# A graph layer's message stage: two tiles of three added on VectorE instead of one of two

## The chip, the cores and the metric

The kernel runs on one core of a Trainium2 chip. The metric is the device time of one execution in microseconds (us), as a median over runs. The engines that matter here are TensorE (PE in the profile; PEld is its weight load), VectorE (DVE), ScalarE (ACT), GpSimd (POOL) and SyncE (SP), which issues transfers.

## The reference

Four blocks follow each other: a relational graph layer pair, a mixture-of-experts block, four graph layers with batch normalization, and a quantized feed-forward block. The change touches the third block alone, of which each layer is

```python
e = edge_attr @ We + be                      # 5000 edges x 512
m = relu(x[src] + e)                         # gather of rows of x, one for each edge
agg = segment_sum(m, dst, num_segments=x.shape[0])
h = ((1.0 + eps) * x + agg) @ W1 + b1
... batch norm, relu, @ W2, relu
```

It runs over 10,000 nodes, 512 features, 5,000 edges, and four layers.

## The kernel before

Each of the four layers is three phases with barriers of all engines between them: `message_phase` (the edges: `m`, and its sums over edges of equal target), `hidden_phase` and `output_phase`. The layers are built as a first one, an inner one that a loop runs twice, and a final one. Edges are sorted by target and cut into `ET` = 40 tiles of 128.

In `message_phase`, for tile t:

- GpSimd gathers 128 rows of the table into `x[t % 8]` (L1820). It waits until tile t-8 has been summed.
- TensorE makes the edge terms in a PSUM bank `X[t % 4]`: a product of 5 rows, `kept_edge_terms` by `kept_attr_terms` (L1904). For a tile that is `summed`, it adds the gathered rows by a second product with the identity matrix (L1912). In the profile that product has two records for each tile.
- For a tile that is not `summed`, VectorE adds bank and gathered rows into an SBUF buffer `z` (`add`, L1849).
- ScalarE takes relu, rounded for TensorE, into `mh` (`high`, L1878). VectorE makes the remainder `ml` (`low`, L1854).
- TensorE multiplies both with a selection matrix into `B` (`sums`, L1920 and L1921), ScalarE copies to `res` (L1883), and SyncE stores `res` and its first and last row (L1804, L1805).

The first layer (`normal`) sums all tiles on TensorE. In the later three, even tiles are `summed`. Every engine works through its own list in program order, which `static_pipeline` writes: at turn t TensorE issues `attr(t)`, then `sums(t - 2)`; VectorE `add(t)`, then `low(t - 1)`; ScalarE `high(t)`, then `result(t - 2)`. TensorE's `sums(t)` waits for `ml` of tile t. After tile 20 ScalarE and after tile 24 VectorE also split the next weights (L717, L721).

`output_phase` of one layer loads the selection matrices and edge terms of the next one ahead, into space that its own big tile has freed. `TERMS_AT`, from `MESSAGE_ROWS`, says from which group of rows on that space is free.

Of the kernel before, what the change touches and what calls it, by code (L numbers as in the profile page):

```python
# [10 lines left out]
P = 128  # L11
N, D, E = 10000, 512, 5000
# [1708 lines left out]
    return v.rearrange(f"one {names} -> (one {names.split()[0]}) {' '.join(names.split()[1:])}")  # L1721


MESSAGE_ROWS = 10
TERMS_AT = (EP + MESSAGE_ROWS * D) - N


# [17 lines left out]
def message_phase(core, ed, table, layer, weight, ident, half, normal, kept, ahead):  # L1745
# [6 lines left out]
    W, R, XR = 4, 8, 4  # L1752
    CHUNK = 5
    HEAD = XR * P
    SPLIT_AT = ET // 2
    summed = lambda t: normal or t % 2 == 0
    of_pe = lambda t: sum(summed(k) for k in range(t + 1))
    of_dve = lambda t: max(0, t + 1) - of_pe(t)
    names = ("w whi wlo terms more sel0 sel1 sel2 sel3 sel4 sel5 sel6 sel7 E X z mh ml B res zero H hres done st0 st1 st2 st3 "
             "bn aggr var rstd nb nx xin swg0 swg1 swg2 swg3 swg4 swg5 swg6 swg7")  # L1760
    with core.phase("message", names) as (s, sbuf, psum):
# [2 lines left out]
        select, edge_terms, attr_terms = kept  # L1764
        sbuf("select", [P, ET, P], F32R)
        x = [sbuf(f"x{q}", [P, D]) for q in range(R)]
        z = [sbuf(f"z{q}", [P, D]) for q in range(2)]
        sbuf("edge_terms", [TERMS, EP], F32R), sbuf("attr_terms", [TERMS, D], F32R)
        borders = sbuf("borders", [EDGE_ROWS, D])
        mh = [sbuf(f"mh{q}", [P, D], F32R) for q in range(W)]  # L1770
# [5 lines left out]
        X = [psum(f"X{q}", [P, D]) for q in range(XR)]  # L1776
        B = [psum(f"B{q}", [P, D]) for q in range(2)]
        H = psum("H", [ET, D])
        ga, st = [s[f"swg{q}"] for q in range(R)], [s[f"st{q}"] for q in range(W)]
        sum_of = lambda t: X[t % XR] if summed(t) else z[t // 2 % 2]  # L1780

        def wait_sum(eng, t):

# [884 lines left out]
def second_gnn(core, cst, ed, a, g, skip, rows_out, stats, rowst):  # L2668
# [3 lines left out]
    with nc.sbuf_tensor("kept_below", [P, 3 * KC, D], F32), nc.sbuf_tensor("kept_select", [P, ET, P], F32R) as select, \  # L2672
            nc.sbuf_tensor("kept_between", [P, MESSAGE_ROWS, D], F32), nc.sbuf_tensor("kept_edge_terms", [TERMS, EP], F32R) as edge_terms, \
            nc.sbuf_tensor("kept_attr_terms", [TERMS, D], F32R) as attr_terms:
        kept = select, edge_terms, attr_terms

    def one_layer(layer, first, final):
        table = skip if first else g
        name = "first" if first else "final" if final else "inner"

        def weight(name):
            return a[name][bass.ds(layer, 1)].rearrange("one (c p) n -> (one p) c n", p=P)

        with nc.sbuf_tensor(f"layer_hi_{name}", [P, KC, D], F32R) as hi, nc.sbuf_tensor(f"layer_lo_{name}", [P, KC, D], F32R) as lo, \
                nc.sbuf_tensor(f"layer_raw_{name}", [P, KC, D], F32) as raw:
            message_phase(core, ed, table, layer, (raw, weight("L1_gnn_W1"), hi, lo), cst.ident, cst.half, first, kept, not first)
            with nc.sbuf_tensor(f"hT_{name}", [P, KC, N], F32) as hT:
                hidden_phase(core, cst, ed, table, a["L1_gnn_eps"], a["L1_gnn_b1"], (raw, weight("L1_gnn_W2"), hi, lo), layer, hT, stats, first)
                affine = a["L1_gnn_gamma"], a["L1_gnn_beta"], a["L1_gnn_b2"]
                if final:  # L2690
                    last_output_phase(core, cst, rows_out, skip, *affine, (raw, hi, lo), layer, hT, stats, rowst)
                else:
                    output_phase(core, cst, ed, g, *affine, (raw, hi, lo), layer, hT, stats, kept)
# [65 lines left out]
```

## Time and profile before

| what | value |
|---|---|
| median of three runs | 4840.01 us (4828.76 to 4846.31) |
| the profiled execution's own time | 4834.37 us |
| its span | 4832.6 us |
| mean granted TensorE clock | 0.897 |
| busy share of PE, DVE, ACT, POOL | 87%, 60%, 43%, 25% |

The three message stages of later layers lie at about 2824 to 2911, 3433 to 3512 and 4030 to 4112 us of the span. A row of a timeline gives start, duration, engine, line, tile names, and in brackets the idle time before it and what ended it. A row of windows gives the busy time of each engine in that stretch, then the granted clock, then the busy share of the transfer engines. A granted clock of 1.00 is 2.4 GHz, and 0.50 is 1.2 GHz, the only two levels seen; a value between them is a mean.

### The profile page before, as it was taken

To read this page: it belongs to the slowest core of one execution; us is meant where nothing else is said; L and a number is where in the kernel's file an instruction comes from. 1 tells how busy PE (TensorE), PEld (TensorE's weight loads), DVE (VectorE), ACT (ScalarE), POOL (GpSimd) and SP (SyncE) were. 2 spreads that over 40 slices of the span, in tenths; PEclk is the share of its full clock that TensorE was granted. 3 is DMA by queue.
4 is the path that set the end of the run, shared out by engine and by line. 5 is a ranking of instruction groups with operands and counts; after the bars stand their busy time and mean duration, and the time that the engine had idled before them with its cause. 6 is when DMAs were issued, how large, how long until landed. Compare 5 with 4: busy or idle time off the path is not lost. (4 is left out here: it accounts for less than half of the span.)

```text
span 4832.6 us, 65959 instructions
## 1 busy us (share of the span) xinstructions
PE 4200.5 (87%) x22921; PEld 3391.4 (70%) x22921; DVE 2883.9 (60%) x6014; ACT 2057.0 (43%) x3499; POOL 1206.0 (25%) x1230
## 2 busy tenths in 40 slices
PE   7868979899898954868899998999889998899967
PEld 4437867778786843653898847988589884898844
DVE  5547743377586766755785444544445444456888
ACT  1212212222233622426556753357533575334556
POOL 2431112211242002875441033300333003330010
PEclk9989989999998966877899989999999998999965
DMA  9982248622598933986442364423655236544677
GB/s 344 399 281 98 74 147 267 223 91 75 200 407 327 346 123 85 175 150 207 150 156 87 117 199 161 163 88 110 212 167 161 85 114 206 168 158 131 186 192 214
DMA packets 454538, 875.49 MB, mean 181 GB/s; under 512 B 69409, under 2 KB 109969, under 8 KB 453486
## 3 DMA queue, kind: packets, MB, share of 16 engines
q1 hardware_dynamic: 305049, 528.82, 32.0%
q0 software_dynamic: 77312, 227.96, 16.7%
q10 hardware_dynamic: 71912, 115.30, 7.1%
q8 instruction: 152, 2.49, 0.2%
q14 instruction: 113, 0.92, 0.1%
HBM read 567.94 MB, written 302.99 MB: 180 GB/s over the span
## 5 line engine op out<-in xcount | busy, mean ns | idle before, releaser
L1974 POOL DMA_INDIRECT hidden_agg<-edge_sums,edge_where x316 | 355.1, 1124 | 702.7 <-DVE layer_raw_inner L2060 288.1
L731 PE MATMUL hidden_O<-hidden_xh,layer_hi_inner 128*128 128x256 f32 (+1 forms) x1280 | 367.9, 287 | 0.0
L733 PE MATMUL hidden_O<-hidden_xl,layer_hi_inner 128*128 128x256 f32 (+1 forms) x1280 | 361.8, 283 | 0.0
L732 PE MATMUL hidden_O<-hidden_xh,layer_lo_inner 128*128 128x256 f32 (+1 forms) x1280 | 361.2, 282 | 0.0
L1820 POOL DMA_INDIRECT message_x<-g,edge_partner x120 | 116.6, 972 | 777.4 <-POOLq L147 461.8
L731 PE MATMUL output_O<-layer_hi_inner,output_hh 128*128 128x512 f32 (+1 forms) x632 | 251.7, 398 | 18.4 <-DVE output_hl L2154 18.4
L2017 ACT ACTIVATE hT_inner<-hidden_O,hidden_b 128x256 f32<-128x256 f32 (+1 forms) x320 | 123.9, 470 | 332.4 <-PE hidden_O L733 332.4
L731 PE MATMUL root_O<-root_hi,root_xh 128*128 128x512 f32 (+1 forms) x632 | 255.8, 405 | 0.0
L731 PE MATMUL relation_B<-relation_weights,relation_pth 128*128 128x512 f32 x640 | 253.7, 396 | 0.0
L732 PE MATMUL relation_B<-relation_weights,relation_ptl 128*128 128x512 f32 x640 | 253.5, 396 | 0.0
L733 PE MATMUL relation_B<-relation_weights,relation_pth 128*128 128x512 f32 x640 | 253.3, 396 | 0.0
L732 PE MATMUL output_O<-layer_hi_inner,output_hl 128*128 128x512 f32 (+1 forms) x632 | 251.3, 398 | 0.0
L733 PE MATMUL output_O<-layer_lo_inner,output_hh 128*128 128x512 f32 (+1 forms) x632 | 251.1, 397 | 0.0
L733 PE MATMUL root_O<-root_lo,root_xh 128*128 128x512 f32 (+1 forms) x632 | 249.0, 394 | 0.0
L732 PE MATMUL root_O<-root_hi,root_xl 128*128 128x512 f32 (+1 forms) x632 | 248.2, 393 | 0.0
L2163 DVE TENSOR_TENSOR layer_raw_inner<-output_O,output_b2t 128x1024 f32<-128x1024 f32 x80 | 96.9, 1211 | 249.9 <-PE output_O L733 249.9
L732 PEld LDWEIGHTS hidden_O<-hidden_xh,layer_lo_inner 128*128 128x128 f32 x1280 | 243.8, 190 | 0.0
L731 PEld LDWEIGHTS hidden_O<-hidden_xh,layer_hi_inner 128*128 128x128 f32 x1280 | 243.5, 190 | 0.2 <-DVE hidden_xl L1104 0.2
L733 PEld LDWEIGHTS hidden_O<-hidden_xl,layer_hi_inner 128*128 128x128 f32 x1280 | 243.5, 190 | 0.0
L1098 ACT ACTIVATE root_xh<-root_T 128x1024 fp32r<-128x1024 f32 x80 | 80.5, 1007 | 348.3 <-PE root_T L987 348.3
L1009 POOL DMA_INDIRECT root_agg<-edge_sums,edge_where x158 | 152.0, 962 | 285.9 <-DVE root_y L1061 173.7
L2072 DVE BATCH_NORM_STATS2 h_stats<-hT_inner 128x6 f32<-128x512 f32 (+2 forms) x168 | 97.6, 644 | 168.4 <-ACT hT_inner L2017 168.4
(464 smaller groups left out, 12723.3 us busy)
## 6 DMA issues: line engine op xcount, KB each, us to landing
edge_sums<-message_res SPq DMA_DIRECT2D x160, 256.0 KB
layer_raw_inner<-g SPq DMA_DIRECT2D x78, 512.0 KB, 3.9
g<-layer_raw_inner SPq DMA_DIRECT2D x78, 512.0 KB
room<-in_L_gnn_basis SPq DMA_DIRECT2D x30, 1280.0 KB, 14.7
order_basis<-in_L_gnn_basis SPq DMA_DIRECT2D x18, 1280.0 KB, 14.2
edge_sums<-relation_res SPq DMA_DIRECT2D x80, 256.0 KB
order_x<-in_x SPq DMA_DIRECT2D x39, 512.0 KB
normed<-order_y ACTq DMA_DIRECT2D x39, 512.0 KB
```

Source lines behind the costliest of these rows:

```text
L731: eng.matmul(out, a_hi, b_hi, start=start, stop=False)
L732: eng.matmul(out, a_lo, b_hi, start=False, stop=False)
L733: return eng.matmul(out, a_hi, b_lo, start=False, stop=stop)
L1009: eng.indirect_dma_start(agg[q][0:n, t, :], None, ed.sums[0], bass.IndirectOffsetOnAxis(ap=ed.where[0][0:n, j:j + 1], axis=0)).then_inc(ga ...
L1098: eng.activation(xh[q][:, :, 0:w], T[q][:, :, 0:w], ACT.Copy).then_inc(s["hi"], 1)
L1820: eng.indirect_dma_start(x[t % R][:, :], None, table, bass.IndirectOffsetOnAxis(ap=ed.partner[1][:, t:t + 1], axis=0)).then_inc(ga[t % R], 16)
L1974: eng.indirect_dma_start(agg[j % R][0:n, :], None, ed.sums[1], bass.IndirectOffsetOnAxis(ap=ed.where[1][0:n, c:c + 1], axis=0)).then_inc(g ...
L2017: m = eng.activation(hT[:, o, at(g)], O[g % 2][:, o, 0:width_of(last(g))], ACT.Identity, bias=b1t[:, o:o + 1])
L2072: eng.bn_stats(stats[:, o, g // 2 + last(g), :], hT[:, o, (g if g in alone else g - 1) * GROUP:at(g).stop]).then_inc(s["bn"], 1)
L2163: eng.tensor_tensor(part(y[q], last), part(O[q], last), b2t[0:n, :].unsqueeze(1).to_broadcast([n, k, D]), ALU.add).then_inc(s["add"], 1)
```

## The change

Of the tiles of later layers only every third is `summed` on TensorE. VectorE adds two of three: 26 tiles instead of 20 in each of the three stages, and TensorE makes 14 identity products instead of 20. A third buffer `z` is added, with its ring counted by the number of adds, and `MESSAGE_ROWS` grows by the one row of space that it takes.

```diff
-MESSAGE_ROWS = 10
+MESSAGE_ROWS = 11
 TERMS_AT = (EP + MESSAGE_ROWS * D) - N
...
-    summed = lambda t: normal or t % 2 == 0
+    summed = lambda t: normal or t % 3 == 0
     of_pe = lambda t: sum(summed(k) for k in range(t + 1))
     of_dve = lambda t: max(0, t + 1) - of_pe(t)
...
-        z = [sbuf(f"z{q}", [P, D]) for q in range(2)]
+        z = [sbuf(f"z{q}", [P, D]) for q in range(3)]
...
-        sum_of = lambda t: X[t % XR] if summed(t) else z[t // 2 % 2]
+        sum_of = lambda t: X[t % XR] if summed(t) else z[(of_dve(t) - 1) % 3]
```

TensorE in the inner layer's message stage before, from `attr(12)` on; the digit behind a name is its buffer, so `X0` is the bank of tiles 12 and 16, and `B0` takes even tiles.

```order
L1904 MATMUL message13_X0<-kept_attr_terms,kept_edge_terms 128x512
L1912 MATMUL message13_X0<-message13_x4,cst_ident 128x512
L1920 MATMUL message13_B0<-message13_mh2,kept_select 128x512
L1921 MATMUL message13_B0<-message13_ml2,kept_select 128x512
L1904 MATMUL message13_X1<-kept_attr_terms,kept_edge_terms 128x512
L1920 MATMUL message13_B1<-message13_mh3,kept_select 128x512
L1921 MATMUL message13_B1<-message13_ml3,kept_select 128x512
L1904 MATMUL message13_X2<-kept_attr_terms,kept_edge_terms 128x512
L1912 MATMUL message13_X2<-message13_x6,cst_ident 128x512
L1920 MATMUL message13_B0<-message13_mh0,kept_select 128x512
```

The same place in the changed kernel:

```order
L1904 MATMUL message13_X0<-kept_attr_terms,kept_edge_terms 128x512
L1912 MATMUL message13_X0<-message13_x4,cst_ident 128x512
L1920 MATMUL message13_B0<-message13_mh2,kept_select 128x512
L1921 MATMUL message13_B0<-message13_ml2,kept_select 128x512
L1904 MATMUL message13_X1<-kept_attr_terms,kept_edge_terms 128x512
L1920 MATMUL message13_B1<-message13_mh3,kept_select 128x512
L1921 MATMUL message13_B1<-message13_ml3,kept_select 128x512
L1904 MATMUL message13_X2<-kept_attr_terms,kept_edge_terms 128x512
L1920 MATMUL message13_B0<-message13_mh0,kept_select 128x512
L1921 MATMUL message13_B0<-message13_ml0,kept_select 128x512
L1904 MATMUL message13_X3<-kept_attr_terms,kept_edge_terms 128x512
L1912 MATMUL message13_X3<-message13_x7,cst_ident 128x512
```

The identity product of tile 14 is gone, and `B0<-mh0`, the sums of the `summed` tile 12, now stand right behind `attr(14)`.

VectorE at the same place before, from the add of tile 13 on (`z0` is tile 13, `ml0` tile 12):

```order
L1849 TENSOR_TENSOR message13_z0<-message13_X1,message13_x5 128x512
L1854 SCALAR_TENSOR_TENSOR message13_ml0<-message13_X0,message13_mh0 128x512
L1854 SCALAR_TENSOR_TENSOR message13_ml1<-message13_z0,message13_mh1 128x512
L1849 TENSOR_TENSOR message13_z1<-message13_X3,message13_x7 128x512
L1854 SCALAR_TENSOR_TENSOR message13_ml2<-message13_X2,message13_mh2 128x512
```

And in the changed kernel, from the add of tile 13 on (`z2` is tile 13, `z0` tile 14):

```order
L1849 TENSOR_TENSOR message13_z2<-message13_X1,message13_x5 128x512
L1854 SCALAR_TENSOR_TENSOR message13_ml0<-message13_X0,message13_mh0 128x512
L1849 TENSOR_TENSOR message13_z0<-message13_X2,message13_x6 128x512
L1854 SCALAR_TENSOR_TENSOR message13_ml1<-message13_z2,message13_mh1 128x512
L1854 SCALAR_TENSOR_TENSOR message13_ml2<-message13_z0,message13_mh2 128x512
```

In both the `low` of the `summed` tile 12 stands behind the add of tile 13. An add of tile 14 is new behind it.

## Rows read from the trace of the kernel before

**Rows 1.** The page: span, and granted clock in 40 slices.

```profile
span 4832.6 us, 65959 instructions
...
PEclk9989989999998966877899989999999998999965
```

**Rows 2.** Windows: the three message stages, from first identity product to last sums.

```profile
2831.00:2910.00 79.00, 76.42 (x159) 32.16 (x159) 41.70 (x61) 46.15 (x80) 33.89 (x36) 0.77 0.77 248
3442.00:3510.00 68.00, 65.12 (x157) 27.75 (x155) 41.55 (x61) 45.13 (x79) 31.93 (x33) 0.91 0.84 280
4035.00:4111.00 76.00, 71.71 (x158) 30.44 (x158) 41.79 (x61) 44.92 (x80) 35.44 (x37) 0.82 0.81 263
```

**Rows 3.** Timeline of PE, two tiles at a granted clock of 1.00.

```profile
3499.31 0.49 PE L1904 MATMUL message_X<-kept_attr_terms,kept_edge_terms 5*128 5x512 f32 x1
...
3500.29 0.79 PE L1920 MATMUL message_B<-message_mh,kept_select 128*128 128x512 f32 x1
...
3501.25 0.50 PE L1904 MATMUL message_X<-kept_attr_terms,kept_edge_terms 5*128 5x512 f32 x1
3501.68 0.50 PE L1920 MATMUL message_B<-message_mh,kept_select 128*128 128x512 f32 x1
...
3502.34 0.49 PE L1904 MATMUL message_X<-kept_attr_terms,kept_edge_terms 5*128 5x512 f32 x1
```

**Rows 4.** Timeline of PE, two tiles at a granted clock of 0.50.

```profile
2842.27 0.79 PE L1904 MATMUL message_X<-kept_attr_terms,kept_edge_terms 5*128 5x512 f32 x1
2842.99 0.80 PE L1920 MATMUL message_B<-message_mh,kept_select 128*128 128x512 f32 x1
...
2844.14 0.79 PE L1904 MATMUL message_X<-kept_attr_terms,kept_edge_terms 5*128 5x512 f32 x1
2844.87 2.08 PE L1912 MATMUL message_X<-message_x,cst_ident 128*128 128x512 f32 x2
...
2847.73 0.79 PE L1904 MATMUL message_X<-kept_attr_terms,kept_edge_terms 5*128 5x512 f32 x1
```

**Rows 5.** Timeline of PE, end of the final layer's stage, after `attr(39)`.

```profile
4108.21 0.49 PE L1904 MATMUL message_X<-kept_attr_terms,kept_edge_terms 5*128 5x512 f32 x1
4108.63 0.50 PE L1920 MATMUL message_B<-message_mh,kept_select 128*128 128x512 f32 x1
...
4110.14 0.50 PE L1920 MATMUL message_B<-message_mh,kept_select 128*128 128x512 f32 x1 [0.77 <-DVE message_ml L1854]
```

**Rows 6.** Timeline of DVE, at the places of rows 5.

```profile
4108.80 0.69 DVE L1849 TENSOR_TENSOR message_z<-message_X,message_x 128x512 f32<-128x512 f32 x1 [1.07 <-PE message_X L1904]
4109.40 0.68 DVE L1854 SCALAR_TENSOR_TENSOR message_ml<-message_X,message_mh 128x512 fp32r<-128x512 f32 x1
```

**Rows 7.** Timeline of DVE, at the places of rows 4.

```profile
2843.16 0.69 DVE L1849 TENSOR_TENSOR message_z<-message_X,message_x 128x512 f32<-128x512 f32 x1 [3.36 <-PE message_X L1904]
2843.76 0.68 DVE L1854 SCALAR_TENSOR_TENSOR message_ml<-message_X,message_mh 128x512 fp32r<-128x512 f32 x1
```

**Rows 8.** Windows: a stretch at either level, inside the first stage of rows 2.

```profile
2832.00:2853.00 21.00, 21.00 (x32) 8.36 (x30) 7.97 (x12) 8.72 (x15) 10.09 (x12) 0.50 0.76 220
2861.00:2872.00 11.00, 10.57 (x30) 4.67 (x29) 7.05 (x11) 7.68 (x15) 6.74 (x8) 1.00 0.97 339
```

**Rows 9.** Timeline of PE, where the granted clock falls in the first stage.

```profile
2878.99 0.50 PE L1920 MATMUL message_B<-message_mh,kept_select 128*128 128x512 f32 x1 [0.43 <-DVE message_ml L1854]
...
2882.98 0.51 PE L1920 MATMUL message_B<-message_mh,kept_select 128*128 128x512 f32 x1 [0.89 <-DVE message_ml L1854]
...
2884.07 1.76 PE L1912 MATMUL message_X<-message_x,cst_ident 128*128 128x512 f32 x2
```

**Rows 10.** Windows: after that fall, and the end of the final layer's stage.

```profile
2885.00:2897.00 12.00, 12.00 (x19) 4.93 (x18) 3.96 (x6) 4.84 (x9) 3.78 (x4) 0.50 0.75 220
...
4104.00:4112.00 8.00, 5.74 (x16) 2.41 (x15) 4.06 (x6) 5.67 (x11) 0.00 (x0) 1.00 0.45 173
```

**Rows 11.** Windows: the first layer's message stage, all tiles summed on PE.

```profile
2191.00:2239.00 48.00, 48.00 (x66) 18.95 (x66) 23.81 (x71) 25.17 (x40) 23.94 (x31) 0.50 0.53 183
2239.00:2291.00 52.00, 51.51 (x134) 22.87 (x133) 41.24 (x120) 46.42 (x79) 31.54 (x42) 1.00 0.72 235
```

**Rows 12.** Timeline of SP's queue, end of an output phase.

```profile
3394.84 0.29 SPq L1738 DMA_DIRECT2D kept_attr_terms<-edge_attr_rows  x1
3399.78 30.05 SPq L2114 DMA_DIRECT2D g<-layer_raw_inner  x7
```

## The prediction

> **What bounds the stage now.** I read the page first, then windows over the three stages that the change touches, then the timelines of TensorE and VectorE inside them. The page gives a span of 4832.6 us and a granted clock that changes from slice to slice [rows 1]. The three message stages of later layers last 79, 68 and 76 us, 223 us in all, 4.6% of the span, so nothing else is at stake [rows 2]. In them TensorE is busy nearly throughout (76.4 of 79 us in the first), VectorE a little over half. TensorE sets the pace: two tiles take 3.03 us at a granted clock of 1.00 (from `attr` at 3499.31 to that at 3502.34) and 5.46 us at 0.50 (2842.27 to 2847.73) [rows 3, 4]. The stages differ in length only by their mean clocks of 0.77, 0.91 and 0.82. Time at 0.50 is twice the missing share: 79 x 2 x 0.23 = 36 us, 12 and 27, together 76 us, or 76 / 2.73 = 28 of 120 tiles. The other 92 at 1.515 us need 139 us. 223 - 76 - 139 leaves 8 us of waits.
>
> **What is removed.** Six identity products in each stage, 18 in all. At 1.00 a tile with one takes 1.94 us (3499.31 to 3501.25) and one without 1.09 (to 3502.34) [rows 3]; at 0.50 it is 3.59 (2844.14 to 2847.73) and 1.87 us (2842.27 to 2844.14) [rows 4]. So a product is worth 0.85 us at the upper level and 1.72 at the lower, and TensorE's own work for three tiles falls from 4.55 to 4.12 us, or from 8.19 to 7.33.
>
> **What is added: a wait at the upper level.** Eighteen adds on VectorE cost 0.69 us each, and VectorE has room. The place decides. `low` of a `summed` tile stands behind the add of the tile after it, which waits for that tile's `attr` product. TensorE's sums of the `summed` tile wait for this `low`. Before, an identity product stood between and hid the detour. Now only `attr` does: from `attr(13)` to `sums(12)` there are one tile without identity (1.09 us) and one `attr` (3501.25 to 3501.68, 0.43), 1.52 us. The trace of before has this pattern once in each stage, at its end, where no identity product follows `attr(39)`. There the add starts 0.59 us after `attr` (4108.21, 4108.80), `low` 0.60 later, it lasts 0.68, and TensorE goes on at 4110.14 [rows 5, 6]: 1.93 us from `attr` to the sums. 1.93 - 1.52 = 0.41 us of waiting in each three tiles, so they take 4.12 + 0.41 = 4.53 us. Before it was 4.55. **At the upper level the gain is nil** (0.02 us for three tiles, under 1 us over all).
>
> At the lower level the add starts 0.89 us after `attr` (2842.27, 2843.16) and `low` 0.60 later [rows 4, 7]; with 0.68 and 0.06 us that is 2.23 us, and TensorE has 1.87 + 0.72 = 2.59 us of its own work in between. No wait: three tiles take 7.33 instead of 8.19 us, a gain of 0.29 us a tile.
>
> The second add and the two `low` behind it end before TensorE needs them, since the next identity product lies ahead. ScalarE's work per tile is unchanged (45 us of 68 busy [rows 2]). Gathers are released by the add or the sum eight tiles earlier, in the same order as before.
>
> Transfers would stop a gain at the upper level even without the wait. Their busy share is 0.97 at 1.00 and 0.76 at 0.50 [rows 8]; at the lower level a tile in 2.44 instead of 2.73 us makes it 0.85, so there is room there.
>
> **The moved loads.** `TERMS_AT` moves the ten loads of the next stage two groups later. Before, seven stores follow the last load, over 30 us (3394.84, 3399.78 to 3429.8) [rows 12]; five will, over some 20 us. They stay hidden behind TensorE's work; uncovered, the delay could cost at most two groups, some 10 us, in three places.
>
> **The clock.** With the clock as before, the sum is 28 x 0.29 = 8 us gained. But the change alters what the clock answers to. In the first stage the clock is 1.00 until TensorE waits 0.43 us and then 0.89 us for `ml`, four microseconds apart; in the next identity product it is 0.50 (the record stretches to 1.76 us), and then it stays there for over 12 us, although TensorE shows no idle time at all [rows 9, 10]. After the change a wait of 0.41 us comes back every 4.53 us through the whole upper level, and the identity product, the longest stretch of unbroken streaming, comes once in 4.53 us instead of once in 3.03. At the lower level it comes once in 7.33 instead of 5.46 us. So I expect it to fall more readily and rise more reluctantly. How reluctant a rise can be shows the first layer: 48 us at 0.50 with TensorE busy without a gap [rows 11].
>
> I put H for the tiles at the lower level. The three stages take 8 + 120 x 1.51 + H x (2.44 - 1.51) us = 189 + 0.93 H. H = 28, as before, gives 215 us, a change of -8. H = 120, never up, gives 301, +78. H = 0 gives -34. Even is H = 37. The rows do not fix H: the fall of rows 9 followed a wait twice as long as the new one, but one such wait and not one every 4.5 us; rises came within 12 us in the second stage (all that it spent at 0.50), after over 21 in the first and after 48 in the first layer [rows 2, 8, 11]. I choose the middle between as before and never up, H = 74: 258 us, +35 us. The profiled execution took 4834.4 us, so 4869 us. Its time lies 6 us under the median shown, inside the runs' spread of 18 us.
>
> The Trainium skill ("TensorE: Matmul & The Clock Gate", section "HAM oscillation") lets the clock fall where matmuls wait long for a transfer and holds it up otherwise; by that rule waits of 0.41 us would cost nothing, and the time would be that of the rival below with the clock as before. The trace disagrees in part: two short waits sufficed. A neighbouring section ("A second HAM failure mode: psum-queue depth-cycling") has short frequent idles between groups of matmuls making it swing, which is my forecast.
>
> **The rivals.**
> - **The clock keeps its pattern.** H stays near 28: -8 us, 4826; with H of 20 to 50, -15 to +13. For it: in the last 8 us of the final stage TensorE is busy for 5.74 us only, with a wait of 0.77 us, and the clock stays 1.00 [rows 10]. Against it: the stretch is short and ends the stage.
> - **The wait does not come, and the clock holds**, the case on the other side. If `low` of the `summed` tile reached TensorE in time, three tiles would take 4.12 us at the upper level, 0.14 us a tile less: 92 x 0.14 = 13 us, with the 8 us of the lower level 21, so 4813 us. It decides if the detour through `attr(13)` is under 1.52 us. Rows 5 and 6 give 1.93, and transfers at 0.97 stand against it too.
> - **The clock never rises.** H = 120, +78 us, 4912. For it: the first layer's 48 us. Against it: all three stages of before rose, with mean clocks of 0.77 and more [rows 2].
>
> **How the numbers follow.** A measurement of this kernel tells about 0.5% from no change, 24 us around 4840. Chances: clock lower for more tiles, H from 50 to 110 (+13 to +68), 0.56; clock as before 0.32; no wait 0.08; never up 0.04. Slower by over 0.5% means over 4864, H above 69: about seven tenths of the first case and all of the last, 0.43. Faster needs under 4816: most of the no-wait case, 0.07. The rest, 0.50, is within 0.5%. The range goes from the clock kept (4826) to H = 110 (4902). The likeliest case alone spans 4847 to 4902.
>
> **What the profile after would show.** At 1.00, TensorE's sums behind the `attr` of a tile t with t mod 3 = 2 wait 0.4 us for L1854, and three tiles take 4.5 us. At 0.50 they take 7.3 us without a wait. The identity product has 82 calls (164 records) in place of 100, VectorE 78 adds in place of 60. The three stages have mean clocks of about 0.65, below 0.77, 0.91 and 0.82. Wrong would be: a clock as before or higher; a wait much shorter than 0.4 us; or a time that moves outside these three stages.

## The result, and the profile after

| | changed kernel | kernel before |
|---|---|---|
| median of nine runs each | 4850.76 us | 4835.16 us |
| ratio (95% interval) | 1.0045 (1.0023 to 1.0067) | |
| mean granted clock of the runs | 0.8937 | 0.8989 (35 later runs) |
| profiled execution, its span | 4842.53, 4840.8 us | 4834.37, 4832.6 us |

The change made the kernel slower by 0.45%, 22 us. The ratio takes in all eighteen runs; their means differ by 21.8 us, the two medians by 15.6. The page of the changed kernel answers to [rows 1]:

```profile
span 4840.8 us, 65941 instructions
...
PEclk9989989999998966888999989999799996999965
```

The windows over its three message stages answer to [rows 2], the last one (the first layer's stage, which the change does not touch) to [rows 11]. Columns as there: after PE, PEld, DVE, ACT and POOL stand the granted clock, the transfer engines' busy share and GB/s.

```profile
2818.00:2893.00 75.00, 68.41 (x147) 28.27 (x146) 44.33 (x67) 45.70 (x80) 34.73 (x35) 0.80 0.82 262
3420.00:3499.00 79.00, 73.24 (x146) 30.34 (x147) 44.47 (x67) 45.95 (x80) 33.94 (x35) 0.74 0.78 246
4027.00:4117.00 90.00, 85.47 (x147) 34.98 (x146) 44.94 (x67) 46.48 (x80) 35.59 (x35) 0.61 0.73 217
2194.00:2275.00 81.00, 80.51 (x198) 34.61 (x197) 64.47 (x188) 69.74 (x118) 54.82 (x73) 0.95 0.78 256
```

The three stages take 75 + 79 + 90 = 244 us in place of 223. Time at 0.50, counted as in the prediction (length x 2 x missing share), is 30 + 41 + 70 = 141 us in place of 76. The span grew by 8 us only, in the main because the first layer's stage, with the same instructions, took 81 us in place of 100: its clock rose sooner in this one execution. So a single pair of profiles misleads here by as much as the effect. The runs do not: over 35 runs of the kernel before, time and mean clock go together (correlation -0.86, 24 us for 0.005 of clock), and the changed kernel's runs lie 0.005 lower.

The timeline of PE in the changed kernel: three tiles at 1.00, the place where the clock falls, and three tiles at 0.50.

```profile
2829.23 0.49 PE L1904 MATMUL message_X<-kept_attr_terms,kept_edge_terms 5*128 5x512 f32 x1
2829.65 1.12 PE L1912 MATMUL message_X<-message_x,cst_ident 128*128 128x512 f32 x2
...
2831.17 0.50 PE L1904 MATMUL message_X<-kept_attr_terms,kept_edge_terms 5*128 5x512 f32 x1
...
2832.26 0.50 PE L1904 MATMUL message_X<-kept_attr_terms,kept_edge_terms 5*128 5x512 f32 x1
2833.11 0.50 PE L1920 MATMUL message_B<-message_mh,kept_select 128*128 128x512 f32 x1 [0.34 <-DVE message_ml L1854]
...
2833.77 0.50 PE L1904 MATMUL message_X<-kept_attr_terms,kept_edge_terms 5*128 5x512 f32 x1
...
2842.34 0.50 PE L1920 MATMUL message_B<-message_mh,kept_select 128*128 128x512 f32 x1 [0.35 <-issue]
...
2843.43 1.64 PE L1912 MATMUL message_X<-message_x,cst_ident 128*128 128x512 f32 x2
...
2849.60 0.79 PE L1904 MATMUL message_X<-kept_attr_terms,kept_edge_terms 5*128 5x512 f32 x1
...
2856.93 0.79 PE L1904 MATMUL message_X<-kept_attr_terms,kept_edge_terms 5*128 5x512 f32 x1
```

Three tiles at 1.00 take 4.54 us (2829.23 to 2833.77), with a wait of 0.34 us for `ml` (VectorE's remainder); at 0.50 they take 7.33 us (2849.60 to 2856.93). The clock falls at 2843.4, in the middle of the plain pattern; in the profile of before each of the three falls came after the weight split [rows 9]. That is not a rule: in `space`, whose stages have the instructions of before, the clock was down in the plain pattern too, behind a longer wait.

```profile
2860.59 0.79 PE L1920 MATMUL message_B<-message_mh,kept_select 128*128 128x512 f32 x1 [2.33 <-DVE message_ml L1854]
```

The timeline of DVE shows why the wait is there: the add of the next tile stands ahead of `low` of the `summed` one.

```profile
2831.76 0.69 DVE L1849 TENSOR_TENSOR message_z<-message_X,message_x 128x512 f32<-128x512 f32 x1 [1.26 <-PE message_X L1904]
2832.37 0.68 DVE L1854 SCALAR_TENSOR_TENSOR message_ml<-message_X,message_mh 128x512 fp32r<-128x512 f32 x1
```

### The profile page after: what moved, and what is told of

Read it like the earlier page. It is cut to its first block and busy times, and to the rows that moved or that the text cites. A ratio compares the mean times of both kernels' runs of the same rounds, so it can differ in the third digit from the quotient of the medians.

```text
span 4840.8 us, 65941 instructions
## 1 busy us (share of the span) xinstructions
PE 4191.8 (87%) x22885; PEld 3381.4 (70%) x22885; DVE 2893.2 (60%) x6032; ACT 2056.4 (42%) x3499; POOL 1206.5 (25%) x1230
```

## The experiments

All ratios are to runs of the kernel before on the same chip in the same session. The expectations weigh two theories. Theory A: the granted clock follows what TensorE streams, and the loss comes from there. Theory B: the clock goes up and down by chance, and the waits or VectorE's adds are the loss. "Stages" is the sum of three windows of one profile, "at 0.50" is counted as above; both scatter, as `space` shows, which has the same instructions in its stages as the kernel before. Outside the three stages the profiles of all these kernels scatter as well, from 4597 to 4640 us, so the ratios of runs decide and not the spans. Mean clocks of runs of the kernel before were 0.8985 to 0.8997.

| run | ratio (95% interval) | clock of runs | stages, us | at 0.50, us |
|---|---|---|---|---|
| `space` | 0.9989 (0.9967 to 1.0010) | 0.8994 | 235 | 101 |
| `after_again` | 1.0049 (1.0024 to 1.0075) | 0.8920 | 237 | 135 |
| `low_first` | 1.0030 (1.0005 to 1.0055) | 0.8928 | 241 | 147 |
| `fill` | 1.0002 (0.9977 to 1.0026) | 0.8980 | 235 | 106 |
| `fill_again` | 1.0000 (0.9981 to 1.0019) | 0.8982 | 221 | 79 |
| `fill_small` | 1.0033 (1.0006 to 1.0060) | 0.8935 | 257 | 164 |
| `fill_small_again` | 1.0048 (1.0026 to 1.0070) | 0.8922 | 237 | 122 |
| `low_first_fill` | 1.0032 (1.0010 to 1.0054) | 0.8946 | 228 | 108 |
| `four` | 1.0076 (1.0050 to 1.0102) | 0.8854 | 256 | 205 |
| `drop` | 1.0076 (1.0050 to 1.0102) | 0.8857 | 253 | 198 |
| `warm_before` | 1.0003 (0.9982 to 1.0025) | 0.9002 | 223 | 66 |
| `full_rows` | 0.9926 (0.9896 to 0.9955) | 0.9035 | 187 | 15 |

**`space`: the room alone.** The kernel before with `MESSAGE_ROWS = 11` and three `z`.

> The kernel before, with only the third buffer z laid out and MESSAGE_ROWS at 11: even tiles are still summed on TensorE, and the loads for the next stage are issued two groups later. Both theories: within 0.2% of the kernel before. A rival (the moved loads cost): up to 10 us in each of three output phases.

No difference beyond the interval: the moved loads cost nothing that shows. Its profile gives the scatter of an unchanged stage, 235 us against 223.

**`after_again`: the change once more.**

> The changed kernel once more, unedited, beside the same runs of the kernel before as the other three, so that they can be compared. Theory A: 0.3 to 0.6% over the kernel before, mean clock of its runs about 0.005 below, three stages 235 to 260 us with over 110 us at 0.50. Theory B: the clock's mean is that of the kernel before over this many runs, and the time within 0.2%.

As theory A says, in ratio, clock, stages and time at 0.50.

**`low_first`: without the wait.**

```diff
+for r in range(ET + 1):
+    first = r > 0 and summed(r - 1)
+    if first:
+        low(r - 1)
+    if r < ET:
+        add(r)
+    if r > 0 and not first:
+        low(r - 1)
...
-static_pipeline([(0, add), (1, low), (1, weight_low)], ET)
```

> The changed kernel, with VectorE's low of a summed tile moved ahead of the add of the tile after it; nothing else moves. Theory A (the granted clock: TensorE streams less in each stretch, through the wait and through the rarer identity product, and so spends more tiles at 0.50): the wait of 0.35 us behind every third attr goes, three tiles at 1.00 take 4.1 to 4.4 us instead of 4.54, and falls of the clock become rarer if the wait drove them: three stages 205 to 230 us in place of 246, time under or at that of the kernel before. If the rarer identity product alone drove the clock, the time at 0.50 stays near 140 us and the stages at 240 us. Theory B (the wait itself is the loss, the clock is chance): the stages lose only the waits, 0.35 us for each three tiles at 1.00, 3 to 6 us in all, and the time at 0.50 is no different.

The timeline of PE shows three tiles in 4.10 us (2861.56 to 2865.66), and no wait behind the third `attr`:

```profile
2861.56 0.49 PE L1913 MATMUL message_X<-kept_attr_terms,kept_edge_terms 5*128 5x512 f32 x1
...
2864.58 0.49 PE L1913 MATMUL message_X<-kept_attr_terms,kept_edge_terms 5*128 5x512 f32 x1
2865.00 0.50 PE L1929 MATMUL message_B<-message_mh,kept_select 128*128 128x512 f32 x1
...
2865.66 0.49 PE L1913 MATMUL message_X<-kept_attr_terms,kept_edge_terms 5*128 5x512 f32 x1
...
2869.97 0.47 PE L1929 MATMUL message_B<-message_mh,kept_select 128*128 128x512 f32 x1 [0.78 <-issue]
```

Yet the clock of the runs is 0.8928, as low as with the change, and 147 us lie at 0.50. So the short wait behind every third `attr` is not needed for the lower clock. Waiting as such was not taken away: four microseconds on, TensorE waits 0.78 us, and later waits last up to 1.7 us. Within the three stages it waits for VectorE 4 us in place of 14, but is idle for 12 us in all, against 17 and 14 in the two profiles of the change.

**`four` and `drop`: more of it, and products or adds.** `four` has `summed = normal or t % 4 == 0`. `drop` is the kernel before, in which tiles with t mod 4 = 2 get neither identity product nor add, so part of the sum is left out; TensorE's list is that of `four`, VectorE's that of before.

```diff
+dropped = not normal and t % 4 == 2
+if dropped:
+    eng.wait_ge(ga[t % R], (t // R + 1) * 16)
...
+if dropped:
+    m.then_inc(s["X"], 1)
+    return
```

> The changed kernel with only every fourth tile summed on TensorE: 10 identity products a stage in place of 14, 30 adds on VectorE. Theory A (streaming of TensorE sets the granted clock): the same direction again, more strongly. A tile at 0.50 takes (3.59 + 3 x 1.87) / 4 = 2.30 us, one at 1.00 about 1.47 (transfers). With four tiles of five at 0.50 the stages take 96 x 2.30 + 24 x 1.47 + 8 = 264 us, time 0.6 to 1.0% over the kernel before, clock below that of the changed kernel. Theory B (adds and waits are the loss, the clock is chance): one wait of 0.35 us in four tiles instead of in three, so the stages are as long as or shorter than with the change, and the mean clock is no lower.

> The kernel before with work left out: of the even tiles, those with t mod 4 = 2 get no identity product and no add either, so their gathered rows are not summed in (10 of 40 tiles in each of three stages). TensorE's list is then that of the run with every fourth tile summed, VectorE keeps its 20 adds. Theory A (TensorE's streaming sets the clock, VectorE's adds cost nothing): clock and time as with every fourth tile summed, mean clock about 0.886, 0.5 to 0.9% over the kernel before, three stages about 255 us with about 200 us at 0.50, although the kernel does less work than before. Theory B (VectorE's adds are the loss): time and clock of the kernel before, or less time.

The windows of `four`:

```profile
2844.00:2930.00 86.00, 80.61 (x139) 33.31 (x137) 47.13 (x71) 46.25 (x80) 35.31 (x35) 0.60 0.75 228
3460.00:3546.00 86.00, 82.01 (x139) 33.76 (x137) 47.14 (x71) 46.45 (x80) 34.62 (x34) 0.58 0.74 226
4072.00:4156.00 84.00, 78.11 (x139) 32.42 (x138) 47.24 (x71) 45.93 (x80) 36.28 (x36) 0.62 0.76 235
```

And of `drop`:

```profile
2826.00:2912.00 86.00, 81.90 (x138) 33.88 (x137) 41.54 (x61) 45.79 (x79) 34.59 (x35) 0.58 0.74 227
3443.00:3528.00 85.00, 80.20 (x139) 33.21 (x138) 41.70 (x61) 45.78 (x80) 33.92 (x35) 0.60 0.74 231
4054.00:4136.00 82.00, 76.13 (x139) 31.31 (x137) 41.54 (x61) 45.63 (x80) 35.62 (x35) 0.65 0.76 240
```

VectorE has 71 operations in a window of the one and 61 in the other. Clocks and lengths agree within the scatter of profiles, and the ratio is the same. So the thirty adds of `four` cost nothing that its interval (0.26% to either side) can show, and the eighteen of the change will not either. Taking ten identity products a stage off TensorE makes the kernel 0.76% slower, even where nobody takes over their work. What `drop` does not tell apart is the missing product and the wait that opens in its place: TensorE waits for `ml` for 13 us in its three stages, as it does in `four` (14 us). That is left to `low_first` and the fillers.

**`fill` and `fill_small`: giving TensorE something back.** The changed kernel with one product into an unused bank behind `attr` of tiles with t mod 3 = 2, of 128 rows, or of 5.

```diff
+if t % 3 == 2:
+    eng.matmul(F[:, :], select[:, t, :], select[:, 0:4, :].rearrange("p a b -> p (a b)"), start=True, stop=True)
```

```diff
+if t % 3 == 2:
+    eng.matmul(F[:, :], edge_terms[:, t * P:(t + 1) * P], attr_terms[:, :], start=True, stop=True)
```

> The changed kernel, with one product of 512 columns into an unused bank behind the attr of each tile t with t mod 3 = 2, where TensorE waits for low. It has no reader. At 1.00 it fits into the wait (0.33 of 0.35 us), at 0.50 it costs 0.60 us for three tiles. Theory A: TensorE streams nearly as much as before the change, so the clock falls less and rises sooner; time at 0.50 near that of the kernel before (76 us in three stages) and the stages 215 to 235 us in place of 246. Theory B (streaming does not matter): time at 0.50 stays near 140 us and each three tiles there take 0.6 us more, stages 250 to 262 us.

> As the run with the filler product, but the filler is a product of 5 rows (the edge terms once more) instead of 128 rows; same place, same columns, same time. Theory A in its plain form (time in which matmuls stream): clock and time as with the 128-row filler, about the kernel before. Theory A2 (a product of few rows does not count, or counts little): clock and time as in the changed kernel without a filler, 0.4% over the kernel before.

> The run with the 128-row filler once more, beside the 5-row filler on the same chip. Theory A: clock about 0.898, time within 0.25% of the kernel before. If the first run was chance: clock 0.892 to 0.894 and 0.3 to 0.5% over, as the changed kernel.

> The run with the 5-row filler once more. If few rows count for little: clock 0.892 to 0.894, 0.3 to 0.5% over the kernel before, and below the clock of the 128-row filler. If rows do not matter: both fillers with the same clock and time.

Both fillers take the same place and keep TensorE's pace at 1.00: 0.84 us from `attr` to the sums, where the changed kernel with its wait has 0.85. First `fill`, then `fill_small`:

```profile
2868.02 0.50 PE L1905 MATMUL message_X<-kept_attr_terms,kept_edge_terms 5*128 5x512 f32 x1
2868.45 0.50 PE L1909 MATMUL message_F<-kept_select 128*128 128x512 f32 x1
2868.86 0.50 PE L1923 MATMUL message_B<-message_mh,kept_select 128*128 128x512 f32 x1
...
2879.67 0.49 PE L1905 MATMUL message_X<-kept_attr_terms,kept_edge_terms 5*128 5x512 f32 x1
2880.01 0.39 PE L1909 MATMUL message_F<-kept_attr_terms,kept_edge_terms 5*128 5x512 f32 x1
2880.52 0.50 PE L1923 MATMUL message_B<-message_mh,kept_select 128*128 128x512 f32 x1
```

In both pairs the 128-row filler brings time and clock back to the kernel before, and the 5-row one leaves them near where the change put them. In the second pair, on one chip, the intervals do not touch. So idle time alone does not explain the lower clock: the 5-row filler closes most of the gap of 0.34 us (0.12 us stays open between the records) and brings nothing back that shows. The fillers differ in more than rows: one multiplies selection matrices, the other edge terms, and at 0.50 the 128-row one takes 1.31 us from `attr` to the sums and the 5-row one 1.15. That the values multiplied matter is not ruled out by this pair; `full_rows`, whose added rows are zero, speaks against it.

**`low_first_fill`.** Both edits together.

> The changed kernel with both edits: low of a summed tile ahead of the next add, and the 128-row filler behind attr of tiles t with t mod 3 = 2. TensorE's own work for three tiles at 1.00 is 4.10 + 0.33 = 4.43 us without a wait for VectorE, against 4.54 of the changed kernel and 4.55 before. Theory A: clock as with the filler alone (time at 0.50 about 110 us in three stages), time within 0.2% of the kernel before. Theory B: only the wait counts, 3 to 6 us less than with the change, whatever the clock.

Missed: 0.32% over, clock 0.8946, where the filler alone had 0.8980. Its interval overlaps that of `fill`, so whether the missing wait matters here stays open.

**`warm_before`: the clock up at the start.** The kernel before with 16 products of 128 rows behind `attr(0)` of the later stages.

> The kernel before, with 16 products of 512 columns into an unused bank at the start of each of the three later message stages, in the some 6 us in which TensorE otherwise waits for the first gather. They have no reader. Theory A: the clock is at 1.00 when the first tile is there, so the stretches at 0.50 at the start (23, 6 and 23 us before) go, and with them 19 tiles' difference of 1.2 us: 15 to 25 us less, stages about 200 us. Theory B (the level is not set by what TensorE streams): the time is that of the kernel before, or a little over if the products delay the first tile.

The clock was at 1.00 at the start, as expected, but not for long. Windows of its first stage, from the first tile on:

```profile
2854.00:2866.00 12.00, 9.85 (x25) 3.66 (x23) 5.95 (x9) 5.19 (x10) 8.22 (x9) 1.00 0.85 266
2867.00:2893.00 26.00, 26.00 (x39) 10.60 (x38) 9.91 (x15) 11.87 (x21) 9.78 (x11) 0.50 0.74 209
```

TensorE was busy for 9.85 of 12 us, then came 26 us at 0.50; the other two stages fell some 15 us after their start as well. The gain expected at the start was given back there, and the expectation of 15 to 25 us less was wrong.

**`full_rows`: a version that beats both.** The kernel before, with `attr` on 128 rows in the later stages; the 123 added rows are zero.

```diff
+nothing = ed.sums[1][ZERO_ROW, :].partition_broadcast(P - TERMS)
+eng.dma_start(edge_terms[TERMS:P, i * D:(i + 1) * D].bitcast(F32), nothing).then_inc(sem, 16)
...
+eng.dma_start(attr_terms[TERMS:P, :].bitcast(F32), nothing).then_inc(sem, 16)
...
-m = eng.matmul(X[t % XR][:, :], edge_terms[:, t * P:(t + 1) * P], attr_terms[:, :], start=True, stop=not summed(t))
+m = eng.matmul(X[t % XR][:, :], edge_terms[0:P if ahead else TERMS, t * P:(t + 1) * P], attr_terms[0:P if ahead else TERMS, :], start=True, stop=not summed(t))
```

> A version meant to beat both. The kernel before (every second tile summed on TensorE), but in the three later message stages the attr product (L1904) streams 128 rows in place of 5: the edge and attribute terms have 123 more rows, all zero, which extra loads in the output phases fill (2.8 MB a layer, where the transfer engines have room). The product has the same 512 columns, so no matmul gets longer. If a product of 128 rows keeps TensorE's clock up where one of 5 rows does not, also where the rows are zero: time at 0.50 in the three stages under 50 us in place of 76 to 103, stages 205 to 220 us, time 0.2 to 0.6% under the kernel before. If zero rows do not help, or rows do not matter: time and clock of the kernel before, within 0.2%, or a little over where the extra loads delay a store.

It is 0.74% faster than the kernel before (0.45 to 1.04%), 4799.01 us against 4830.43, and more than was expected (0.2 to 0.6%). Windows of its three stages, and of 20 us within the first:

```profile
2843.00:2908.00 65.00, 53.30 (x159) 29.20 (x157) 41.88 (x61) 44.58 (x80) 35.68 (x35) 0.94 0.88 302
3437.00:3499.00 62.00, 51.83 (x157) 27.82 (x156) 41.35 (x61) 43.91 (x79) 35.42 (x35) 0.96 0.92 316
4026.00:4086.00 60.00, 50.75 (x159) 28.02 (x157) 41.97 (x61) 44.36 (x80) 34.87 (x35) 0.98 0.92 325
...
2860.00:2880.00 20.00, 16.94 (x54) 9.34 (x54) 12.51 (x19) 14.63 (x26) 13.87 (x14) 1.00 1.01 361
```

Its timeline of PE, with the one fall of the clock inside that stage, from the second row to about 2902:

```profile
2863.22 0.47 PE L1923 MATMUL message_B<-message_mh,kept_select 128*128 128x512 f32 x1 [0.85 <-ACT message_res L1886]
...
2898.55 0.64 PE L1923 MATMUL message_B<-message_mh,kept_select 128*128 128x512 f32 x1 [2.91 <-ACT message_res L1886]
...
2902.27 0.39 PE L1907 MATMUL message_X<-kept_attr_terms,kept_edge_terms 128*128 128x512 f32 x1
2902.50 0.40 PE L1923 MATMUL message_B<-message_mh,kept_select 128*128 128x512 f32 x1
2902.74 0.39 PE L1924 MATMUL message_B<-message_ml,kept_select 128*128 128x512 f32 x1
2902.97 0.40 PE L1907 MATMUL message_X<-kept_attr_terms,kept_edge_terms 128*128 128x512 f32 x1
```

Two things changed at once. The clock is up nearly throughout, although TensorE now idles 9 to 12 us in each stage, in place of 3 to 4 [rows 2]. And the products stand closer: from `attr` to the sums 0.23 us in place of 0.43 at 1.00 [rows 3]. The second gives next to nothing at 1.00: a tile still takes 1.5 us there, with the transfers at a share of 1.01, and by the prediction's sum the stages of before would last 8 + 120 x 1.515 = 190 us with the clock up throughout, where `full_rows` has 187. That the transfers hold the tile is argued from their share alone. The closer spacing may well be part of why the clock holds. Rows and spacing were not told apart here. The fillers come nearer to that, since at 1.00 both leave 0.84 us from `attr` to the sums.

## Why the prediction was right, and where its size was off

- **The three tiles.** Forecast 4.53 us at 1.00 with 0.41 us of wait, and 7.33 at 0.50 with none; measured 4.54, 0.34 and 7.33. The end of each stage in the kernel before did show the new wait.
- **The clock.** The sign was right and carried the result: over the three stages the mean clock fell from 0.83 to 0.71 in the first profile, though the first stage, at 0.80 against 0.77, went the way that was named as a sign of being wrong. The term H was too large: 74 tiles at the lower level, against 141 / 2.44 = 58 in the first profile and 135 / 2.44 = 55 in the second. The formula holds (189 + 0.93 x 58 = 243, measured 244). That gives +21 us in place of +35, and the runs say 22. The middle between two ends was a choice, not a reading; that it came out this near is in part luck. The end "as before" was also a single draw: `space` had 101 us at 0.50, 37 tiles, where the profile of before had 76. So the match of 21 and 22 is luck too: the two profiles of the change have 244 and 237 us for the stages, those of before and `space` 223 and 235, which is 11.5 us on average.
- **Its reason was half right.** I named two: the repeated wait, and the rarer identity product. `low_first` has the low clock without the repeated wait; `drop`, together with the fillers, points to the missing 128-row products. The passage of rows 9, where the clock fell after two waits, had suggested the wait.
- **VectorE's adds and the moved loads at nothing:** right within the intervals (`drop` against `four`, `space`).
- **The page's rule.** By the Trainium skill ("TensorE: Matmul & The Clock Gate", section "HAM oscillation") the clock should fall at long waits. The trace of `full_rows` agrees: waits of 0.85 us and up to 2.02 us passed, and after 2.91 us it was at 0.50 for some 3 us. In the changed kernel the trace disagrees: it fell at 2843.4 with no wait above 0.51 us in the 20 us before.

## What to carry to other kernels

Work taken off TensorE can cost time: here ten products fewer a stage cost 0.76%, through the clock. Read the granted clock of the stage, and price the change at both levels before counting the saved products. An idle slot on TensorE can be worth filling, and a product over few rows worth widening with zeros; one kernel shows it here, so try it before relying on it. Where one level is reached or missed by chance, compare the clocks of many runs; one pair of profiles can show the opposite.

## What was not expected of the hardware

- A product of 5 rows is dearer in its surroundings than one of 128 with the same columns: where each tile has a 5-row product, `attr` and the two sums start 0.33 to 0.43 us apart at 1.00 [rows 3], and 0.23 us apart in `full_rows`, where all have 128 rows. The Trainium skill (same page, section "LDWEIGHTS (loading the stationary operand)") has the weight load depend on columns and not on rows. The load records agree with it (at 1.00, 0.18 us for 5 rows before and 0.19 for 128 in `full_rows`), so the spacing comes from somewhere else; no run here shows from where.
- A filler product of 5 rows did nothing that shows for the granted clock, one of 128 rows brought it back: 0.892 against 0.898 in runs on one chip, which differ in the filler alone, its rows and its operands.
- The adds of ten tiles a stage more on VectorE, and ten products fewer on TensorE, moved the time by nothing that shows and by +0.76%.
